# A two-layer feature-interaction kernel: pairs of quarters evicted together, two blocks per DMA, and another prologue

## The reference

```python
B, M, D = 2048, 39, 16          # x: (B, 39, 16), W0: (1, 39*39, 128), W1: (1, 39*128, 128)
x0 = xk = x
outs = []
for W in (W0, W1):
    Hk = xk.shape[1]            # 39, then 128
    Wr = W.reshape(39, Hk, 128)
    xk = einsum('bid,bjd,ijh->bhd', x0, xk, Wr)
    outs.append(xk)
return sum(concatenate(outs, axis=1), axis=-1)      # (B, 256)
```

## Time and profile before

| | |
|---|---|
| median of 3 runs | 618.28 us (617.67 to 619.59) |
| the profiled execution | 613.03 us, span 610.8 us, mean granted clock 0.989 |
| busy: PE, DVE, ACT, POOL | 557.6 (91%), 466.3 (76%), 465.6 (76%), 462.1 (76%) us |
| DMA queue q1 | 149.94 MB, 73.0% of 16 engines |
| first matmul | at 12.32 us |
| block copies xbd<-xdhl | 512 DMAs of 20 KB |

### The profile page before, as it was taken

The page is one execution under the profiler, slowest core; times in us unless marked ns, Lnnn a source line. Parts: engine busy times, 40 slices in busy tenths (PEclk is TensorE's granted clock), DMA queues, the critical chain, the costliest instruction groups (busy, mean ns, idle before and its releaser), DMA issues.

```text
span 610.8 us, 12886 instructions
## 1 busy us (share of the span) xinstructions
PE 557.6 (91%) x3176; PEld 484.1 (79%) x3176; DVE 466.3 (76%) x806; ACT 465.6 (76%) x980; POOL 462.1 (76%) x404
## 2 busy tenths in 40 slices
PE   1768889999999999999799989999999899999978
PEld 0556767888888888888688878878888788888877
DVE  4858788888888778977678878778978778788630
ACT  4678788888888778877588877778888778888730
POOL 5979899788877787777677877787788678878600
PEclk9979899999999999999999999999999999999999
DMA  8989988877787677777767777687768777878100
GB/s 300 322 315 318 321 291 287 273 258 252 242 279 260 237 260 258 235 253 276 222 228 238 245 261 255 215 281 260 240 240 273 268 240 249 283 256 279 54 30 18
DMA packets 71029, 150.76 MB, mean 247 GB/s; under 512 B 14256, under 2 KB 31024, under 8 KB 70960
## 3 DMA queue, kind: packets, MB, share of 16 engines
q1 hardware_dynamic: 70960, 149.94, 73.0%
HBM read 137.30 MB, written 4.65 MB: 232 GB/s over the span
## 4 chain that ended last, share of the span: by engine, by line
PE 41%; SPq 25%; DMA 11%; issue 8%; POOL 6%; ACT 5%; DVE 4%; ACTq 0%; DVEq 0%; POOLq 0%
SPq L269 16%; DMA xs<-xa_dram 10%; PE acc L359 7%; PE acc L361 6%; PE acc L360 6%; SPq L238 4%; PE fin L399 3%; PE fin L400 3%; PE fin L401 3%; POOL fl L688 3%; PE pg L385 3%; PE pg L386 3%; PE pg L387 3%; POOL fs L683 2%; ACT fh L452 2%
## 5 line engine op out<-in xcount | busy, mean ns | idle before, releaser
L688 POOL TENSOR_TENSOR fl<-fs,fh 128x512 fp32r<-128x512 f32 x192 | 247.5, 1300 | 90.7 <-ACT fh L452 90.6
L359 PE MATMUL acc<-fh,w0h 128*128 128x512 f32 x384 | 164.8, 429 | 39.5 <-ACT x L473 25.8
L584 DVE TENSOR_TENSOR fp<-xl,xr 128x512 f32<-128x512 f32 x192 | 133.5, 696 | 63.5 <-ACT xl L459 54.1
L683 POOL TENSOR_TENSOR fs<-xr,xs 128x512 f32<-128x512 f32 x128 | 163.0, 1292 | 8.2 <-DMA xr<-xb_dram 6.8
L361 PE MATMUL acc<-fl,w0h 128*128 128x512 f32 x384 | 153.6, 400 | 0.0
L360 PE MATMUL acc<-fh,w0l 128*128 128x512 f32 x384 | 152.7, 398 | 0.0
L588 DVE TENSOR_TENSOR fl<-fp,fh 128x512 fp32r<-128x512 f32 x192 | 131.4, 685 | 22.9 <-ACT fh L452 21.0
L602 DVE TENSOR_TENSOR gl<-pg,gh 128x320 fp32r<-128x320 f32 x256 | 118.9, 486 | 30.8 <-ACT gh L492 27.5
L452 ACT ACTIVATE fh<-fp 128x512 fp32r<-128x512 f32 x192 | 114.3, 595 | 33.3 <-PE acc L361 31.2
L452 ACT ACTIVATE fh<-fs 128x512 fp32r<-128x512 f32 x192 | 121.5, 633 | 18.8 <-PE acc L361 15.1
L492 ACT ACTIVATE gh<-pg 128x320 fp32r<-128x320 f32 x256 | 106.3, 434 | 22.2 <-PE pg L387 21.5
(11 more groups left out here) (38 smaller groups left out, 684.6 us busy)
## 6 DMA issues: line engine op xcount, KB each, us to landing
xr<-xb_dram SPq DMA_DIRECT2D x192, 512.0 KB, 5.7
xs<-xa_dram SPq DMA_DIRECT2D x64, 256.0 KB, 4.7
xbd<-xdhl SPq DMA_DIRECT2D x512, 20.0 KB, 3.6
xp<-xpairs_dram SPq DMA_DIRECT2D x32, 256.0 KB, 2.8
xdr<-xd_dram SPq DMA_DIRECT2D x64, 80.0 KB, 2.5
w_copy<-w_dram SPq DMA_DIRECT2D x6, 384.0 KB, 5.6
w1l<-w_copy SPq DMA_DIRECT2D x6, 384.0 KB, 4.4
out_dram<-outs SPq DMA_DIRECT2D x8, 256.0 KB, 5.8
```

The source lines that it names most:

```text
L359: nc.tensor.matmul(acc[:, :], w0h[:, t, :], fh[:, t, :], start=t == 0, stop=False)
L584: nc.vector.tensor_tensor(f_at(t), xl[:, :], xr[:, gi % 2, t, :], ALU.mult).then_inc(prod_dve, 1)
L683: nc.gpsimd.tensor_tensor(f_at(t), xr[:, gi % 2, t, :], xs[:, gi % 2, :], ALU.mult)\
L688: nc.gpsimd.tensor_tensor(fl[:, t, :], f_at(t), fh[:, t, :], ALU.subtract).then_inc(low_pool, 1)
```

## The change

- **Pairs of quarters.** pg becomes one buffer for two quarters (16 b, 64 columns apart, 40 used). PE does six matmuls for a pair, then ACT evicts 640 elements at once and DVE subtracts 640. The second pair of a group waits until DVE is done with the first. It now stands behind tile 2 instead of in front of it.
- **Two b per DMA.** The host lays xd out with zeros so that 32 partitions can be copied with two b at a time: four DMAs of 80 KB instead of eight of 20 KB. xd's load and its two splits are twice as large. xdr has one buffer, xdhl still two.
- **x first.** SP waits for product 4 and loads xs right away, before the blocks; xd is loaded at the end of a group's list, behind the wait for POOL's split of the group before.
- **w1** comes straight from DRAM into `outs` as a one-piece buffer: ten pieces of four rows, in groups 0 to 9. The load of a piece waits for the low part of the piece before. The second layer waits only for the pieces it uses.
- **POOL** does low 5 of a group behind the products 1 and 4 of the next.
- **Prologue.** w0's second part is loaded and split later, the first tiles' products come sooner.

```diff
-        xdr = sb("xdr", [P, 2, NQ, MI])
-        xdhl = sb("xdhl", [P, 2, NQ, 2, MI], F32R)
+        xdhl = sb("xdhl", [P, 2, 2, NQ, 2, MI], F32R)     # xdr stays [P, 2, NQ, MI], now one buffer
-        pg = ps("pg", [P, 2, GC])
+        pg = ps("pg", [P, BU, BSTEP])                      # BU = 16, BSTEP = 64
 # SP
             def w1_load(p):
-                sp.wait_ge(w1_moved, 16 * (p + 1))
                 if p:
-                    sp.wait_ge(w1_in, 16 * p)
-                sp.dma_start(w1l[:, piece(p), :].bitcast(F32), w1_copy[:, piece(p), :]).then_inc(w1_in, 16)
+                    sp.wait_ge(w1_ready, p)
+                sp.dma_start(w1_raw(p), w1[:, piece(p), :]).then_inc(w1_in, 16)
-                for b in range(BQ):
-                    rows = slice(D * b, D * b + D)
+                for b in range(0, BQ, 2):
+                    rows = slice(D * b, D * b + 2 * D)
...
-                    sp.wait_ge(xd_low, g + 1)
                     if more3:
                         wait_product(sp, g + 1, 0)
-                        wait_product(sp, g + 1, 1)
+                        wait_product(sp, g + 1, 4)
+                        load_x(j, gi + 3)
                         load_right(j, gi + 3, 0)
                     blocks(g, gi, first)
-                    if more2:
-                        load_xd(g + 2, gi)
                     if gi % 2 == 0 and more2:
                         sp.wait_ge(sq_ready, CP * j + gi // 2 + 1)
                         load_pair(CP * j + gi // 2 + 1)
                     if more3:
                         wait_product(sp, g + 1, 3)
                         load_right(j, gi + 3, 1)
-                    if first and gi < PIECES:
-                        w1_load(gi)
-                        if gi + 1 < PIECES:
-                            w1_move(gi + 1)
                     if more3:
-                        wait_product(sp, g + 1, 4)
-                        load_x(j, gi + 3)
                         wait_product(sp, g + 1, 5)
                         load_right(j, gi + 3, 2)
+                    if not (last and gi + 1 >= CB):
+                        sp.wait_ge(xd_low, g + 2)
+                    if more2:
+                        load_xd(g + 2)
+                    if first or second and g + 1 < PIECES:
+                        w1_load(g + 1)
...
 # SP, prologue: behind the wait for product 5 of group 0
-            w1_move(0)
+            sp.wait_ge(xd_low, 1)
+            load_xd(1)
+            sp.wait_ge(w0_sum, 1)
+            w1_load(0)
 # PE
+            def g_pair(j, gi, u, fresh):
+                if u == 0:
+                    pe.wait_ge(x1t_low, g + 1)
+                    pe.wait_ge(xbd_in[s], 16 * (BQ // 2) * nth(j, gi))
+                if not fresh:
+                    pe.wait_ge(g_low, NPAIR * g + u)
+                for q in (2 * u, 2 * u + 1):
...
                     main(j, gi, 0, fresh)
                     main(j, gi, 1, fresh)
+                    main(j, gi, 2, fresh)
                     if not (first and gi < 2):
-                        for q in (2, 3):
-                            g_tile(j, gi - 2, q, False)
-                    main(j, gi, 2, fresh)
+                        g_pair(j, gi - 2, 1, False)
 # ACT
             def xd_split(j, gi, fresh):
-                act.wait_ge(xd_in[gi % 2], 16 * nth(j, gi))
+                act.wait_ge(xd_in, 16 * (g + 1))
                 if not fresh:
-                    act.wait_ge(xbd_in[gi % 2], 16 * BQ * (nth(j, gi) - 1))
+                    act.wait_ge(xbd_in[gi % 2], 16 * (BQ // 2) * (nth(j, gi) - 1))
...
                     if prev:
                         turned_high(g - 1)
                     if more:
                         xd_split(j, gi + 1, first and gi == 0)
+                    if (first or second) and 0 < g <= PIECES:
+                        w1_high_part(g - 1)
+                    if more:
                         high(g + 1, 4, False)
                         high(g + 1, 3, False)
 # DVE, prologue: product 0, low 0, products 2 and 3, low 2 now stand before w0's second part, then
+            product(0, 0, 5, True)
             dve.wait_ge(w0_high, 2)
             nc.vector.tensor_tensor(w0l[:, W0_PART:NT, :], two, w0h[:, W0_PART:NT, :], ALU.subtract)
+            low(0, 3)
             dve.wait_ge(w0_high, 4)
 # POOL
-                    low(g, 5)
                     if more:
                         product(j, gi + 1, 1, False)
                         product(j, gi + 1, 4, False)
+                    low(g, 5)
+                    if more:
                         low(g + 1, 1)
                         xd_split(g + 1, gi + 1)
+                    if (first or second) and 0 < g <= PIECES:
+                        w1_low_part(g - 1)
+                    if more:
                         low(g + 1, 4)
```

## The result

The changed kernel takes **669.12 us**, median of 4 runs (668.29 to 673.11), against 618.93 (617.67 to 620.03) for the kernel before; the ratio is 1.0824, 95% interval 1.0774 to 1.0874. Predicted were 634.6 us, with a range of 617 to 651. The direction was right, the size was not. The profiled execution took 668.29 us; its span is 666.1 us and its mean granted clock 0.928.

What follows compares the result with a forecast made beforehand. TensorE was taken as the bound, 8.43 us a group (8.64 in the loop). 28.5 - 14.3 + 2.1 = +16.3 us on the profiled 613.03 gave 629.3, or 634.6 on the medians' scale; range 617 to 651.

Steps and rivals of the forecast that it cites:

- The circle: First ten groups: SP's w1 load waits for w1 low, behind xd's split; rounds of 12.1 us, +28.5 us at x1_out(10).
- xd's landing: In each round of the first groups, xd lands 9.3 us after SP began; bounds 7.85 and 11.65.
- x1_out(0): Group 0's copy of acc into x1, after the reordered prologue: at about 25.0 us instead of 22.98.
- The steady part: Groups behind the tenth: four block copies relieve SP, xs is no longer late, 14.3 us saved; pairs cost nothing.
- covered by 0.7 us: Second pair's wait for the single pg buffer: ready after 2.2 us, PE asks at 2.9, so hidden.
- still some 0.8 before it is wanted: DVE's turned_low, needed by the next first pair, comes about 0.8 us later yet some 0.8 us before PE wants it.
- The tail: End of the kernel: pairs cannot alternate between pg buffers, 5.7 us against 3.96, turned_low 0.4 later: +2.1 us (0 to +3).
- Circle doesn't bind: First ten groups: w1_low is done before SP comes to the wait; -15.7 us, 602.6 us; chance 0.10.
- xd lands as fast as alone: First ten groups: xd lands in 2.5 us despite the queue; round 10.6, +2.8 us, 621 us; chance 0.13.
- The clock rival: First ten groups: PE's idling drops it to half clock; round 13.9, +32.5 us, 651 us; chance 0.07.
- The last rival: Steady groups: something other than xs holds x1_out as long, so no 14.3 us gain; 649 us; chance 0.04.
- the second rival: First ten groups: SP's w1 wait doesn't bind, GpSimd limits at 8.7 us; x1_out(10) at 110.9, 602.6 us; chance 0.10.

Runs made afterwards that it cites:

- e1: The changed kernel, with SP asking for each w1 piece one group later: 617.72 us, 1.0029 of the kernel before.
- e2: The changed kernel, with xd's load issued right behind the w1 wait, ahead of xs, xr and blocks, in groups 1 to 9: 647.74 us.
- e9: e1 with the second layer evicted by quarters, as in the kernel before, instead of pairs: 608.06 us, 0.9871 of the kernel before.
- e10: e9 with the prologue order of the kernel before: 604.18 us, 0.9790 of the kernel before.
- e12: e1, pairs kept, with the prologue order of the kernel before: 614.77 us, 0.9974 of the kernel before.
- e6: The kernel before with two b per DMA, one xdr buffer and xd loaded at the end of the list: 612.01 us, 0.9899 of before.
- e8: e4 with the second pair moved in front of tile 2: 627.64 us, 1.0184 of the kernel before.
- e4: The kernel before with pairs of quarters alone, second pair behind tile 2: 625.07 us, 1.0166 of the kernel before.
- e5: The kernel before, with SP waiting for product 4 and loading xs ahead of the eight block copies: 618.72 us, 1.0038 of before.
- e7: e6 with xs also loaded first, by the two lines of e5: 628.32 us, 1.0174 of the kernel before.
- e11: e10 with xs loaded after the right halves and low 5 ahead of the next products on GpSimd: 604.90 us, 0.9812 of before.

## Why the prediction was wrong, step by step

The forecast for one execution was 629.3; it took 668.29. The 39.0 us between them are 26.3 up to x1_out(10), 9.3 behind it and 3.4 in the tail. Median against median the miss is 34.5: the prediction built on an execution 5.3 us under its kernel's median, the new one is 0.8 under.

**The circle: right.** Its members, their order, ACT's x1_out behind it (2.9 us after the split's start, 3.0 predicted) and what SP waits for are as written, and e1 takes it away with one line. SP's issuing was 4.9 us (5.35 predicted), splits and w1 low 2.7 (2.8).

**The failed term: xd's landing.** I let xd land 3.95 us after its issue, by dividing the round's 2.66 MB through 386 GB/s, the rate of one full stretch. It was in use 7.0 us after its issue. In 67.5 to 79.5 us the queue moved 2.59 MB at a busy share of 0.79 and 216 GB/s. Per busy share this is some 273 GB/s, against some 382 in the stretch I took; besides, the DMA engines were not busy throughout, 0.64 from 68 to 70 us, while SP was still issuing, and 0.17 from 78 to 80. The queue's backlog was visible: xr took 6.3 us to land, and that was my own upper bound for xd behind it (11.65 instead of 9.3, a round of 14.4). The measured round is 14.57. I took a value from the best rate where the row for the same queue in the same groups stood beside it. Nine rounds at 2.47 more are 22.2 us.

By the fit in the Trainium skill (DMA: Bandwidth & Descriptors, Anatomy of one DMA), 2.0 us plus bytes over 436 GB/s, 160 KB are an estimate of 2.4 us; the page gives it for single DMAs issued by GpSimd, here SP issues. The trace comes near it for an xd in front of the queue, 2.8 us in e2, and not for one behind 1 MB, 6.8.

**The range.** With the round at its own upper bound, 14.4, the forecast was 634.6 + 9 × 2.3 = 655; my range ended at 651 although it should have taken in the bounds of the unknown costs.

**x1_out(0)**, 29.04 instead of 25.0: I followed w0_ready 3, product (1,4) and low(0,5), and these came within about a microsecond of where I had them (L658 at 15.80, product at 21.01). What I left out is that xd(1) has no second buffer now and is issued behind them, at 19.48, and that x1_out(0) is queued behind its split. The order costs 2.3 us at x1_out(0) (e9 and e10) or 3.4 (e1 and e12), in the medians 3.9 and some 3, each with overlapping intervals. PE's first matmul came at 9.57 us instead of 12.32 and gained nothing.

**The steady part: half right.** Two b per DMA gives 10.5 of the 14.3 us (e6), and e10 has 11.6 (458.5), both held against the short execution of the kernel before. The pairs take 5.8 back (e10 and e12). The step that failed is not "covered by 0.7 us": the second pair was covered, as e8 shows from the other side. It is "still some 0.8 before it is wanted", said of turned_low. DVE's queue is in order, and the first pair's low part can begin only when ACT has the whole 640: DVE stands 82.5 us for ACT's high part in e12, against 33.7 in e10. So everything behind it on DVE moves later against PE. For turned_low PE waits 21 times (13.5 us) in place of 7. Where it is not covered is seen in a group with squares; DVE, POOL and PE:

```profile
604.07 1.54 DVE L593 TENSOR_TENSOR sq<-xp,sq 64x512 fp32r<-64x512 f32 x1
605.64 0.82 DVE L603 TENSOR_TENSOR gl<-pg,gh 128x640 fp32r<-128x640 f32 x1
...
607.58 0.68 DVE L598 TENSOR_TENSOR x1tl<-turn,x1th 128x512 fp32r<-128x512 f32 x1
```

```profile
603.77 1.30 POOL L686 TENSOR_TENSOR fl<-fs,fh 128x512 fp32r<-128x512 f32 x1 [0.68 <-ACT fh L456]
```

```profile
599.17 0.40 PE L359 MATMUL acc<-sq,w0q 128*128 128x512 f32 x1
...
607.60 0.39 PE L359 MATMUL acc<-sq,w0q 128*128 128x512 f32 x1
608.32 0.42 PE L392 MATMUL pg<-xbd,x1th 128*128 128x320 f32 x1 [0.33 <-DVE x1tl L598]
...
616.54 0.40 PE L359 MATMUL acc<-sq,w0q 128*128 128x512 f32 x1
```

The squares' low part (L593) takes 1.54 us there; in the four such groups of the kernel before between 500 and 560 us it takes 0.69. Later by that, turned_low ends when PE already asks. On PE itself, from one L359 to the next, the step without the wait is the old 8.43 us and the step with it is 8.94; x1_out, queued on ACT, spreads this to 8.61 and 8.78. The traces bear the link out: from 170 us on, in the changed kernel, e1, e12 and e4, PE waits 0.3 to 0.9 us for turned_low behind each squares' low part of 1.5 us or more, and behind none of 0.69 (in the changed kernel 13 and 13 of 26). In e12 there are 13 such steps behind group 10, at some 0.5 us each, which is about the 5.8. In a group without squares turned_low starts 2.87 us behind the turn (612.25 to 615.12) where it was 2.03 (562.97 to 565.00): that is the predicted delay of 0.8, and it is covered. The term put at nothing is the 0.85 us by which the squares' low part grew. No run removes that alone.

The 9.3 us are so 5.8 from the pairs and 3.5 more. Of these, 1.2 is the step to x1_out(11), 9.82 us, still behind the circle. e10, which has no such step, needs 2.7 more than the predicted 455.8 too (470.1 - 14.3), in single steps of 9 us and more; their cause stays open.

**The evictions**, 701 and 825 ns (680 and 850 predicted), and POOL's split, 879 (880): right.

**The tail**: +5.5 instead of +2.1. From the first pg to the second layer it is 7.0 us, not 5.7, and turned_low is 0.9 later instead of 0.4. The remainder, 1.6 us, lies in the second layer itself. The failed step is that all of it was counted at full clock. PE's idles between the pairs are 1.65 us, about the predicted 1.7, but the second pair's matmuls took 1.97 us where 1.15 was put; in e1 the first pair still has the full clock and takes 2.82 with its idle, as predicted (2.85). The granted clock was 0.50 (1.2 GHz) from 640.5 to 650. Is that the price of the pairs' longer idles? Not alone. The kernel before, e9 and e10, with idles of 1.41, 0.61 and 1.05, had 1.00 throughout, but e5 has the same idles and falls to half clock too:

```profile
593.38 0.41 PE L384 MATMUL pg<-xbd,x1th 128*128 128x320 f32 x1 [1.41 <-DVE x1tl L596]
...
595.15 0.51 PE L384 MATMUL pg<-xbd,x1th 128*128 128x320 f32 x1 [0.61 <-DVE gl L601]
...
598.05 0.58 PE L398 MATMUL fin<-gh,w1h 128*128 128x256 f32 x1 [1.05 <-DVE gl L601]
```

```profile
595.20:599.00 3.80, 2.75 (x10) 2.35 (x11) 1.32 (x3) 0.88 (x2) 0.72 (x1) 0.52 0.00 0
```

So do e7 and e11, and e6 in part. With quarters the tail is 26.3 us at full clock (before, e9, e10), 27.6 in e6 and 28.7 at half (e5, e7, e11); with pairs it is 30.9 to 32.0, at half clock in all seven kernels. Of the 5.5 us some 2.4 are so the clock, which kernels without pairs pay as well, and some 3.1 the pairs at the same clock.

**The rivals.** "Circle doesn't bind" and "xd lands as fast as alone" are out by the round of 14.57. The clock rival's round, 13.9, came near the measured one by luck: PE ran at 0.50 in the first 5 us of the round, behind an idle of 5.71 us, and then at 1.00. Its last product for acc began at 76.54 us, 5.9 before x1_out, which stood on ACT behind xd's split; so the clock did not set the round. The last rival, that something else holds x1_out as long, is seen in e5, where x is moved without fewer DMAs; in the changed kernel 5.0 of the 14.3 us came. Two small slips changed nothing: the floor of the 53 groups adds up to 451.35, not 451.2, and the 110.9 of the second rival has no starting time beside it.

Together, by the ratios to the kernel before, each in its own group of runs: taking the circle away (after to e1) is worth 8.0% of its time, some 49 us, the old prologue (e1 to e12) 0.5%, some 3, quarters instead of pairs (e12 to e10) 1.8%, some 11. What is left of the change, two b, w1 straight from DRAM and x first with low 5 behind, gains 2.1%, some 13 us. By spans the four are 47.7, 4.4, 10.5 and 7.3, the last again held against the short execution of the kernel before.

## What to carry to other kernels

For each wait that an edit puts into an in-order queue, ask for the whole path from what is queued behind it to what releases it. If the path leads through a load in the same queue, every round costs the queue's full latency, and asking for the same transfer one step later can be the whole cure. Price a load behind others by the landing of its neighbours in the same stretch (6.3 us here), not by its own landing alone or by the best rate seen. Fewer, larger evictions from one buffer save engine time that was free; they lengthen the hand-over and move whatever stands behind them in an in-order queue, and it is worth a look at what that then runs beside. Before you read a difference of a few us from two traces, see where each profiled execution lies among the runs of its kernel.

## What the runs showed of the hardware that was not expected

- **Rate of a full queue.** The same queue moved 386 GB/s at a busy share of 1.01 and 242 at 0.95 in the round (the stretch 68.5 to 73.5 above). Both have block copies and xr in flight. In 2 us pieces of the round it is 221 to 241 GB/s from 70 to 76 us, at 0.95 to 1.10 busy, and 337 at 0.88 from 76 to 78. What makes a busy engine slower there was not taken apart.
- **VectorE beside GpSimd.** sq low is DVE's only subtraction in the groups with both inputs in SBUF. It takes 0.69 us alone and up to 1.83 beside POOL's. In the case above POOL's L686 began 0.3 us before it and ended at 605.07; 0.54 us later DVE was done. In the 17 places of the changed kernel where a single row shows the end of a POOL instruction that was running when it began, it ended 0.54 to 0.56 us behind that end. It goes the other way too: where sq low began first, it took 0.69, and L686, begun within it, 1.83 to 1.85 in 11 of 13 places instead of 1.3. In the mean it is 764 ns before, 857 in e10, 1083 after and 1131 in e12: the pairs shift it onto POOL's instruction. The Trainium skill (SBUF — State Buffer, Who interferes with whom) says that a DVE instruction with two SBUF inputs contends with a GpSimd instruction that reads SBUF, and that the order of issue decides which of them is blocked. The trace agrees in both directions, with these numbers.
- **The clock in the tail.** Idles of the same length in the same place (1.41, 0.61 and 1.05 us) went with full clock in three kernels and with half clock in three others. In e5 the clock fell at about the second pg, behind an idle of 0.61 us. What decides between the two is open.
